# V for three images per group, bias spread by transfers, fp32 token blocks and own-half score waits in a ViT tower on one core

## What is computed

```python
x = jnp.einsum('bnf,df->bnd', x, W_lin) + b_lin        # 36 patches of 768 values -> 256
h = concat([cls, x], axis=1) + position_embeddings       # 16 images x 37 tokens x 256
n = layernorm(h)
q, k, v = shape(n @ w_q), shape(n @ w_k), shape(n @ w_v) # 16 heads of 64
scores = einsum('bhqd,bhkd->bhqk', q, k) + rel_bias_table[bucket(k - q)]
h = h + (softmax(scores) @ v) @ w_o
# then: 7 routed experts (top 2) and a shared one; a scan over tokens; a gated channel mix
```

## Time and profile before

| | |
|---|---|
| median of 3 runs | 336.63 us (335.09 to 336.87) |
| profiled execution, its own time | 338.75 us |
| its span | 336.9 us |
| PE busy | 323.3 us, 96% |
| DVE busy | 208.4 us, 62% |
| ACT busy | 192.9 us, 57% |
| POOL busy | 145.0 us, 43% |
| bytes moved | 44.42 MB, mean 132 GB/s |

### The profile page before, as it was taken

How to read it: one execution, slowest core, us unless ns; L and a number is a source line. 1 busy time by engine, 2 the same in 40 slices (tenths; PEclk the granted TensorE clock), 3 DMA queues, 4 the chain that set the end, 5 groups by cost and what they waited for, 6 DMA issues and landing times.

```text
span 336.9 us, 7603 instructions
## 1 busy us (share of the span) xinstructions
PE 323.3 (96%) x3230; PEld 298.5 (89%) x3230; DVE 208.4 (62%) x367; ACT 192.9 (57%) x321; POOL 145.0 (43%) x102
## 2 busy tenths in 40 slices
PE   8999999999999999988999998999999999999895
PEld 8976877899998999977999998999999999986574
DVE  2677233565564596648855858484948497645863
ACT  3783233756545686436578556565756654468660
POOL 3043012385441424453665653746656586200132
PEclk9999999999999999999999999999999999999999
DMA  7937450004000621556565647566565563000002
GB/s 276 406 110 236 131 211 0 6 2 128 4 2 4 183 68 64 178 189 219 184 201 164 201 156 224 182 194 212 177 210 156 156 238 99 21 1 3 0 0 77
DMA packets 31042, 44.42 MB, mean 132 GB/s; under 512 B 1618, under 2 KB 19346, under 8 KB 31004
## 3 DMA queue, kind: packets, MB, share of 16 engines
q1 hardware_dynamic: 28412, 39.89, 36.4%
q0 software_dynamic: 960, 2.43, 2.2%
q10 hardware_dynamic: 1632, 1.57, 1.4%
HBM read 38.22 MB, written 5.49 MB: 130 GB/s over the span
## 4 chain that ended last, share of the span: by engine, by line
PE 81%; DVE 10%; ACT 6%; issue 2%; POOL 0%; ACTq 0%; DVEq 0%; POOLq 0%
PE ps L1454 20%; PE ps L1456 19%; PE ps L1455 19%; PE ps L1781 5%; DVE c_region L916 3%; PE ps L1486 3%; PE ps L1586 3%; PE ps L1613 3%; DVE w_lo L916 2%; PE ps L1462 2%; PE ps L1479 2%; PE ps L1571 1%; ACT w_hi L643 1%; DVE s_region L1250 1%; ACT x_squared L561 1%
## 5 line engine op out<-in xcount | busy, mean ns | idle before, releaser
L1454 PE MATMUL ps<-c_region,w_hi 128*128 128x256 f32 (+2 forms) x312 | 92.3, 296 | 1.8 <-DVE s_region L1250 1.1
L1455 PE MATMUL ps<-c_region,w_hi 128*128 128x256 f32 (+2 forms) x312 | 89.6, 287 | 0.0
L1456 PE MATMUL ps<-c_region,w_lo 128*128 128x256 f32 (+2 forms) x312 | 89.6, 287 | 0.0
L409 POOL TENSOR_TENSOR w_lo<-w_stage,w_hi 128x1024 fp32r<-128x1024 f32 x15 | 44.7, 2978 | 48.7 <-ACT w_hi L643 48.7
L1454 PEld LDWEIGHTS ps<-c_region,w_hi 128*128 128x128 f32 x312 | 59.5, 191 | 3.0 <-DVE s_region L1250 1.5
L1455 PEld LDWEIGHTS ps<-c_region,w_hi 128*128 128x128 f32 x312 | 59.5, 191 | 0.2
L1456 PEld LDWEIGHTS ps<-c_region,w_lo 128*128 128x128 f32 x312 | 59.5, 191 | 0.0
L916 DVE TENSOR_TENSOR c_region<-s_region,c_region 128x512 fp32r<-128x512 f32 (+1 forms) x44 | 47.8, 1086 | 18.1 <-ACT c_region L771 11.9
L643 ACT ACTIVATE w_hi<-w_stage 128x1024 fp32r<-128x1024 f32 (+1 forms) x42 | 49.6, 1192 | 4.4 <-DVE v_region L1304 4.4
L1454 PE MATMUL ps<-xn_hi,w_hi 128*128 128x296 f32 x128 | 40.1, 313 | 1.5 <-DVE s_region L1143 1.5
L1456 PE MATMUL ps<-xn_hi,w_lo 128*128 128x296 f32 x128 | 38.2, 299 | 0.0
(11 more groups left out here) (177 smaller groups left out, 633.4 us busy)
## 6 DMA issues: line engine op xcount, KB each, us to landing
w_stage<-in_w_gate SPq DMA_DIRECT2D x17, 512.0 KB, 3.7
w_stage<-in_w_up SPq DMA_DIRECT2D x17, 512.0 KB, 4.2
w_stage<-in_w_down SPq DMA_DIRECT2D x8, 1024.0 KB
expert_rows<-zeros SPq DMA_DIRECT2D x1, 1792.0 KB, 13.8
v_region<-in_patches SPq DMA_DIRECT2D x3, 576.0 KB, 6.2
v_region<-expert_rows SPq DMA_DIRECT2D x1, 1536.0 KB, 7.2
expert_out<-v_region ACTq DMA_DIRECT2D x6, 256.0 KB, 4.2
w_stage<-in_w_v SPq DMA_DIRECT2D x1, 1024.0 KB, 8.1
```

What stands on the lines that cost most here:

```text
L409: g.tensor_tensor(piece(wl, n), piece(ws, n), piece(wh, n).bitcast(F32), ALU.subtract).then_inc(lo_e[n], 1)
L1454: mm(o, a_h, b_h, start=start, stop=False)
L1455: mm(o, a_h, b_l, start=False, stop=False)
L1456: return mm(o, a_l, b_h, start=False, stop=stop)
```

## The change

- Inputs: W_lin and the patches are one tensor `blocks`, and each of the six feature blocks comes with one transfer. The constants come in two parts, the small one (one-hot bias columns) before the weights, the rest after.
- Tokens: the first two blocks (`FULL`) are multiplied in plain fp32, without a split; four blocks keep the three passes. 9 instead of 15 matmuls on zeros, which start when `zeros` is set.
- Bias: one matmul gives 16 heads x 73 relative positions; a transfer writes each head's row 48 times to DRAM (`bias_rows`), and two transfers of 48 rows read it back, shifted by one element per row.
- V: groups of three images, all used. Groups 0 and 1 have 111 rows, group 2 has two images (74 rows) and lands in the free `x_squared` or `x_centred`. Transfers of 48 rows (`move_values`) put the images where the context matmuls read them; PE waits for them (`d_vm`) at the transposes of step 2 and 3. The very first V half is one fp32 product (`value_full`) and needs no split.
- DVE's list: the split of the second half's xn and of w_k and w_q now stand between V copies.
- Scores of a step wait for the q and k of their own half.
- Token weights of expert 2 are worked out after its y copy.

```diff
 HID = 1024
 KH = HID // P
 E = 7
...
-            return v_all[0:VR, pair * INNER + n * 512:pair * INNER + (n + 1) * 512]
+        def v_rows(g):
+
+            return VR if g % VG < 2 else T2
+
+        def v_half(g, n):
+
+            c, i = g // VG, g % VG
+            if i == 2:
+                return (sq, xc)[c][0:T2, n * 512:(n + 1) * 512]
+            o = (c * PPC + 3 * i) * INNER + n * 512
+            return v_all[0:VR, o:o + 512]
+
+        def v_rows_of(pair, r0):
...
+        def v_bank(g, n):
+
+            return 2 * (g % 2) + n if g < VG else 2 + n
...
-            for i in range(3):
-                for o, x, n in ((wlin_s, w_lin, KF * D // 3), (patch_s, patches, PW // 3)):
-                    sp.dma_start(o[:, i * n:(i + 1) * n], x[:, i * n:(i + 1) * n]).then_inc(d_patch[i], 16)
+            for k in range(KF):
+                r = slice(k * FB, (k + 1) * FB)
+                sp.dma_start(vreg[:, r], blocks[:, r]).then_inc(d_patch[k], 16)
             sp.dma_start(pb[:], par).then_inc(s["d_par"], 16)
-            sp.dma_start(cb[:], const).then_inc(s["d_const"], 16)
+            sp.dma_start(cb[:, 0:CB_ID], const[:, 0:CB_ID]).then_inc(s["d_oh"], 16)
...
+            sp.dma_start(cb[:, CB_ID:CB], const[:, CB_ID:CB]).then_inc(s["d_const"], 16)
+            sp.wait_ge(s["bias_ev"], 1)
+            sp.dma_start(brows.rearrange("h (q r) -> h q r", r=REL),
+                         pat(bias_t, 0, [0, MR], [1, REL])).then_inc(s["d_brows"], 16)
+            sp.wait_ge(s["d_brows"], 16)
+            sp.wait_ge(s["gap_set"], 1)
+            for b2 in range(2):
+
+                sp.dma_start(bias[b2 * RT:b2 * RT + MR, :].rearrange("q (h k) -> q h k", k=T),
+                             bass.AP(brows.tensor, brows.offset + T - 1, [[REL - 1, MR], [MR * REL, HEADS], [1, T]])
+                             ).then_inc(s["d_bias"], 16)
             sp.wait_ge(w_lo[2], 1)
             sp.wait_ge(s["up_lo"], 1)
+            sp.wait_ge(s["v_mm"], 1)
             sp.dma_start(part(2).rearrange("p (k n) -> p k n", k=HP), rows(w_o, HP)).then_inc(d_w[2], 16)
 
...
+            def move_values(c):
+
+                p = c * PPC
+                for i in range(2):
+                    sp.wait_ge(s["v_ev_act"], VG * c + i + 1)
+                    sp.wait_ge(s["v_ev_dve"], VG * c + i + 1)
+                    to, of = (0, T) if i == 0 else (VR - MR, T2 - MR)
+                    sp.dma_start(v_rows_of(p + 1 + i, to), v_rows_of(p + 3 * i, of)).then_inc(d_vm[c], 16)
+                sp.wait_ge(s["v_ev_act"], VG * c + VG)
+                sp.wait_ge(s["v_ev_dve"], VG * c + VG)
+                for i in range(2):
+                    sp.dma_start(v_rows_of(p + 1 + i, T2 * (1 - i)),
+                                 (sq, xc)[c][i * T:i * T + MR, 0:INNER]).then_inc(d_vm[c], 16)
+
+            move_values(0)
+            sp.wait_ge(s["v_pad"], 2)
+            move_values(1)
...
+            g.memset(zero[:], 0.0).then_inc(s["const_set"], 1)
             g.memset(ones[:], 1.0 / D).then_inc(s["const_set"], 1)
-            g.memset(zero[:], 0.0).then_inc(s["const_set"], 1)
             g.memset(eps[:], EPS).then_inc(s["const_set"], 1)
             for a in (xnf, xh, xl):
                 g.memset(pat(a[:], N, [NT, KD], [1, NT - N]).bitcast(F32), 0.0).then_inc(s["pad_set"], 1)
             g.memset(bias[0:QR, :], 0.0).then_inc(s["gap_set"], 1)
             g.memset(sreg[0:QR, 0:3 * SC], 0.0).then_inc(s["gap_set"], 1)
+            for pair in (PPC + 1, PPC + 2):
+                g.memset(v_all[0:VR, pair * INNER:(pair + 1) * INNER], 0.0).then_inc(s["v_pad"], 1)
...
+            for k in range(FULL, KF):
+                act.wait_ge(d_patch[k], 16)
+                for o, x, n in ((wh, wlin_s(k), D), (patch_h, patch_s(k), B * NP)):
+                    a.activation(o[:, k * n:(k + 1) * n], x, ACT.Copy).then_inc(s["tok_hi"], 1)
...
+            def v_evac(g):
+                act.wait_ge(s["v_mm"], 2 * g + 1)
+                a.activation(v_half(g, 0), ps[0:v_rows(g), v_bank(g, 0), :], ACT.Copy).then_inc(s["v_ev_act"], 1)
+
+            for g in range(VG):
+                v_evac(g)
...
+                if t == 0:
+                    v_evac(VG)
+                    v_evac(VG + 1)
+                if t == 1:
+                    v_evac(VG + 2)
...
+                dve.wait_ge(s["bias_mm"], 1)
+                v.tensor_copy(bias_t, bank(5, REL)[0:HEADS, :]).then_inc(s["bias_ev"], 1)
                 dve.wait_ge(w_hi[2], 1)
                 w_low(2, INNER)
-                for c in range(C):
-                    normal(L, c)
-                    low(L, c)
-                    if L == 0 and c == 0:
-
-                        dve.wait_ge(s["bias_mm"], 1)
-                        v.tensor_copy(pat(bias_q[0:T, :], 0, [T, HEADS], [1, 32]),
-                                      pat(ps[0:T, 1, :], 0, [1, HEADS], [HEADS, 32])).then_inc(s["bias_ev"], 1)
-                        v.tensor_copy(pat(bias_q[0:T, :], 32, [T, HEADS], [1, T - 32]),
-                                      pat(ps[0:T, 3, :], 0, [1, HEADS], [HEADS, T - 32])).then_inc(s["bias_ev"], 1)
+                normal(L, 0)
+                low(L, 0)
+                normal(L, 1)
...
+
+            def v_evac(g):
+                dve.wait_ge(s["v_mm"], 2 * g + 2)
+                v.tensor_copy(v_half(g, 1), ps[0:v_rows(g), v_bank(g, 1), :]).then_inc(s["v_ev_dve"], 1)
+
+            v_evac(0)
+            low(0, 1)
+            v_evac(1)
+            dve.wait_ge(w_hi[1], 1)
+            w_low(1, W1 // 2)
+            dve.wait_ge(w_hi[0], 1)
+            w_low(0, W1 // 2)
+            v_evac(2)
...
-                    if e == 2:
-                        token_weights()
-                        dve.wait_ge(s["comb_set"], 2)
-                        choice_weights()
                     if final:
                         piece_low("u0", NX)
                     low(3)
@@ -1302,6 +1350,10 @@
                         dve.wait_ge(d_y[e % 2], 16 * ((e - 1) // 2))
                     o = (e % 2) * G + D
                     v.tensor_copy(y_s[:, o:o + D], bank(5, D)).then_inc(s["y_ok"], 1)
+                    if e == 2:
+                        token_weights()
+                        dve.wait_ge(s["comb_set"], 2)
+                        choice_weights()
 
...
-            pe.wait_ge(s["const_set"], 3)
-            keep_clock(15)
-            for k in range(KF):
-                pe.wait_ge(s["tok_lo"], 2 * k + 2)
+            pe.wait_ge(s["const_set"], 1)
+            keep_clock(9)
+            for k in range(FULL):
+                pe.wait_ge(d_patch[k], 16)
+                for i, (m, c) in enumerate(MC):
+                    mm(bank(4 + i, NPC), wlin_s(k)[:, m * P:(m + 1) * P], patch_s(k)[:, c * NPC:(c + 1) * NPC],
+                       start=(k == 0), stop=False)
+            for k in range(FULL, KF):
+                pe.wait_ge(s["tok_lo"], 2 * (k - FULL) + 2)
                 for i, (m, c) in enumerate(MC):
                     w_ = slice(k * D + m * P, k * D + (m + 1) * P)
                     x_ = slice(k * NP * B + c * NPC, k * NP * B + (c + 1) * NPC)
                     w = three(bank(4 + i, NPC), wh[:, w_], wl[:, w_], patch_h[:, x_], patch_l[:, x_],
-                              k == 0, k == KF - 1)
+                              False, k == KF - 1)
...
+            mean(0, 0)
+            mean(0, 1)
+            pe.wait_ge(s["d_oh"], 16)
             pe.wait_ge(s["d_table"], 16)
-            for k in range(T):
-                lhs = cb[0:BUCKETS, CB_OH + T - 1 - k:CB_OH + 2 * T - 1 - k]
-                w = mm(ps[0:T, 1 + 2 * (k // 32), (k % 32) * HEADS:(k % 32 + 1) * HEADS], lhs, tb[0:BUCKETS, :],
-                       start=True, stop=True)
-            w.then_inc(s["bias_mm"], 1)
-
+            mm(ps[0:HEADS, 5, 0:REL], tb[0:BUCKETS, :], cb[0:BUCKETS, CB_OH:CB_OH + REL],
+               start=True, stop=True).then_inc(s["bias_mm"], 1)
+            variance(0, 0)
+            variance(0, 1)
+
+            def value_full(pair, n):
+
+                i = pair // 2 * 4 + pair % 2
+                for k in range(KD):
+                    w = mm(ps[0:VR, v_bank(pair, n), :], xnf[:, k * NT + i * T:k * NT + i * T + VR],
+                           ws[:, 2 * W1 + k * INNER + n * 512:2 * W1 + k * INNER + (n + 1) * 512],
+                           start=(k == 0), stop=(k == KD - 1))
+                w.then_inc(s["v_mm"], 1)
...
+            def value(g, n):
+
+                if g >= 2:
+                    held = 2 if g < VG else 1
+                    pe.wait_ge(s["v_ev_act"] if n == 0 else s["v_ev_dve"], g - held + 1)
+                o = (g // VG * 8 + (0, 5, 3)[g % VG]) * T
+                for k in range(KD):
+                    x_h, x_l = (x[:, k * NT + o:k * NT + o + v_rows(g)] for x in (xh, xl))
+                    w_ = slice(2 * W1 + k * INNER + n * 512, 2 * W1 + k * INNER + (n + 1) * 512)
```

(80 more changed lines are left out.)

60 lines of the change are left out of this document (18 added, 42 removed).

## The result

The changed kernel takes 326.77 us (median of 4 executions, 326.00 to 328.52) beside 336.29 for the kernel before (4 executions, 335.09 to 336.87): ratio 0.9735, 95% interval 0.9712 to 0.9757. The forecast was 326.7 in 324.0 to 332.0. The profiled execution took 328.52, with a span of 326.1 us against 336.9. The ratios in this text are the recorded estimates over all executions and differ a little from the quotient of two medians (0.9717 here). Executions more than 1.5% above the fastest of the same kernel are left out of ratios and medians, and are named where they occur.

A forecast was written before the change was run, and what follows sets the result against it. TensorE, busy 96% of the span, was taken as the bound. Terms 5.3 + 0.7 + 0.65 + 2.8 + 0.5 = 9.95 us took 338.75 to 328.8, scaled to 326.7 us; range 324 to 332.

The forecast's parts named there:

- Tokens, 15.75: Token blocks on TensorE, two in fp32 with one transfer per block, end at 15.75 instead of 16.91; gain 0.95 us.
- V first half, q and k at 31.05, scores at 34.35: First-half V products end at 30.7; q and k start at 31.05 instead of 36.38, scores at 34.35 instead of 40.40.
- The terms that add to 8.8: Gains up to the first transposes: 5.3 to q and k, 0.7 at first scores, 2.8 in V's second half.
- Rival 1: VectorE bounds the V stage: weight splits beside GpSimd take 2.11 us each, q and k start 1.9 later; 328.6, chance 0.22.
- Own half, 0.7 and 0.65: Scores waiting only for their own half's q and k gain 0.7 us at the first scores, 0.65 over five later steps.
- Bias, cost 0: Bias-row transfers to DRAM and back land about 28, before VectorE needs them at 34.8; no cost up to 87 ns a piece.
- rivals 2 and 3: Bias transfers moderately late (chance 0.08 part of gain lost, 0.03 slower), or partly on one engine, some 50 us slower (0.01).
- Rival 4: The front's gain is given back because a later stage waits for a load; 334 or so, chance 0.04.
- V moves, cost 0, bounds 0 and 2: The second half's last V-row transfer lands at 50.5, before TensorE wants it at 51.2; cost 0, at most 2 us.
- The zero fill shifted, cost 0: Zero fill, w_o and gate loads shift behind the V moves on SP, the last to about 56; ScalarE wants them after 100.
- Token weights, 0.5: Moving expert 2's seven small VectorE operations behind the y copy removes a 0.50 us TensorE wait at 191.60; gain 0.5.
- Sum: All gains together, 9.95 us, take the profiled 338.75 to 328.8, scaled to a median of 326.7.

The follow-up runs named there:

- the second profile: The changed kernel run again unchanged and profiled; 329.6 us over four executions, ratio 0.9784 to the kernel before; the profiled execution took 333.72 us.

## Why the prediction was right, and where it was not

**Tokens, 15.75.** 16.2 in this profile, 14.9 to 16.5 over those with fp32 blocks. Right, with a scatter of over 1 us that lies in the first 10 us: sixteen records of fp32 blocks took from 4.05 to 5.13.

**V first half, q and k at 31.05, scores at 34.35.** 31.76 and 35.20: the order of waits as forecast (VectorE's split of w_q, 0.65), late by the tokens' 0.4 and by small sums. The first transposes at 49.06 against 48.1; 48.47 with a quick start. The terms that add to 8.8 measured 7.9, and 8.5 with the quick start. Rival 1 did not occur: the two splits took 2.35 together.

**Own half, 0.7 and 0.65.** 1.4 when undone (1.2 by the ratios). Right.

**Bias, cost 0.** Right: released by the scores, at 35.87. Written rows landed about 5 us after their issue; rivals 2 and 3 are out. The pieces of 292 B were indeed slower than those of 512 B: at the 70 GB/s of 21 to 23 us a piece takes an estimated 67 ns on its engine (292 B x 16 / 70 GB/s) against 28, still below the 87 from which it would have cost. And 0.79 of the 16 engines were busy then, against 0.07 with 37 rows. What the term left out is the clock that the removed matmuls can bring down (above). Rival 4, a gain given back later to a wait for a load, happened in small, and at a place where it had named none: the V moves.

**V moves, cost 0, bounds 0 and 2. This step failed.** I took "lands at 50.5; PE wants it at 51.2" from the 2.0 us of one transfer. The last of the moves took 4.65 from issue to landing (4.77 in the second profile), so TensorE waited 2.11 (2.23), more than the upper bound; and the bound had only the wait in it, not the clock that fell behind it, 1.5 more. Put where V is read, the same wait costs nothing. The text named "transposes of the second half released by the V moves" as what would prove it wrong, and that is what stands in the trace.

**The zero fill shifted, cost 0.** It wasn't free: with fills back in the early place the kernel is 2.0 us faster than the changed kernel beside it (0.9723 against 0.9784), though only 0.4 faster than in the first comparison. 1.0 to 1.1 of it is a shorter wait. The rest goes to the clock and to the gaps of the loaded stretch, in shares that the runs do not give. I asked only who waits for those transfers, not what runs beside them.

**Token weights, 0.5.** Mis-sized: 1.7 to 2.5. The delay was added up, but not what it leads to: VectorE's split comes behind the start of GpSimd's, and a second wait of 1.10.

**Sum.** 9.95 was forecast with moves that cost nothing. The variant in which they do cost nothing, and the fills stand early, is at 0.9699; the forecast's ratio is 326.7/336.63 = 0.9705. Even this agreement holds 1.2 to 2 us more from the token weights than forecast and as much less from the rest. In the changed kernel itself the loss, 3.7 us in the profiled execution, was made up by 1.2 to 2 at the token weights and, on the executions first compared, by fewer disturbances than later: 0.9735, then 0.9784. That 326.77 lies so near to 326.7 is luck.

## What to carry to other kernels

Put a wait for a transfer in front of the first instruction that reads it, not at the top of the step: here 2.2 us of work stood behind the wait that did not need it, and it is what hides the transfer. Price a wait on TensorE with the slow clock that may follow it, and price a delayed VectorE instruction by what GpSimd may have started ahead of it. And compare two profiles at many checkpoints before believing that a matching total confirms its terms: a 3.8 us difference between them lay in a stage that the change doesn't touch.

## What the runs showed of the hardware

- TensorE's clock fell to 0.50 after pauses of 2.11, 2.23, 1.73 and 2.57 us and after an issue gap of 1.62, and did not after pauses of 1.14, 1.45 and 1.48 or gaps of 0.93, 1.22 and 1.24. Once it fell without a pause just ahead, behind 74 records of 16 columns; in two other profiles the same records left it at 1.00. Each fall lasted some 3 to 4 us.
- Issue gaps of 0.93 to 1.62 us on TensorE, inside groups without a semaphore between, at 67.6, 67.6, 70.7 and 76.5 us. In all four profiles the DMA engines were 0.74 to 0.94 busy over the 4 us before, and 0.00 to 0.22 in the gap; other profiles have such a stretch and no gap. The changed kernel's profile counts instruction loads as transfers of their own (26 packets, 0.43 MB). That they queue behind that traffic would fit, and wasn't tried by itself.
- VectorE's gap ahead of one gate multiply near 140 us: the step takes 3.3 to 6.2 us in thirteen of fourteen profiles and 2.4 in one. Its cause is open.
- VectorE's fp32 split of 128x1024 took 1.22 us when it started 0.39 ahead of GpSimd's, and 3.42 when it started 0.20 behind it, ending 1.08 after GpSimd's end.
- Moves of 192 KB: the last pair took 3.0 to 5.1 us from issue to landing over eleven profiles, with zeros, with weights or with nothing behind them; over all eight moves of a profile it was 2.7 to 6.8.
